# Order of TensorE's work in the steady steps of a window-attention kernel: attention groups ahead of first-layer groups, and one small product moved up

## The chip, the cores and the metric

The kernel runs on one core of one Trainium2 chip. The metric is the device time in microseconds. Before the change it was 338.09 us, the median of 3 runs (336.73 to 339.00).

## The reference, cut to what matters

The input is 8 images of 128 channels by 32 by 32 in float32. Two blocks follow one another.

- The first is a window transformer block. Each image is cut into 16 windows of 8 by 8 tokens. Tokens are normalised over the channels, projected to queries, keys and values for 8 heads of width 16, and softmax attention runs inside each window; its output is projected and added to the input. Then every token is normalised again, goes through a two-layer perceptron (128 to 256, silu, 256 to 128), and the result is added.
- The second is a linear attention block over all 1024 tokens of an image: q, k and v of width 64, `(q k) / N` times v with no softmax, an output projection and the input added. Since nothing non-linear stands between these products, the kernel works with a matrix M of 128 by 128 for each image, made from keys and values, and a column d: the output is M times the tokens plus d.

## The kernel before, in words

The work unit is half an image: 512 tokens, 8 windows, treated as four pairs of windows p = 0 to 3. A step handles several halves at once: half b is in its attention, half a (the next) in its projections, next_a in its first normalisation, half c (the one before) in its output projection, second normalisation and first layer, and the half called tail in its second layer and its keys and values. An even step has b on the first half of an image, an odd step on the second. The loop runs seven even steps of the common form (`even_step`) and six odd ones (`odd_step`), after a prologue and a first and second step of their own, and ahead of an epilogue. Image products of stage d (the matrix M and the output) run in odd steps, for the image before.

Each engine has its order of work written out by hand, one function for each step and engine. Within an engine all is in order; between engines there are only semaphores. The orders of ScalarE (lines 1330 and 1352), GpSimd (600 and 611) and SP (458 and 466) are of the same kind as those that the change touches, TensorE's (983 and 1010) and VectorE's (1690 and 1722).

The names that matter:

- `b_score` (TensorE, 739): scores of all four pairs, for the row maxima. In an even step it stands behind a wait for the first output half to be read from its bank, at the end of the odd step's list.
- `b_scoreT(b, p)` (TensorE, 765): transposed scores of pair p, six products in fp32r and four bfloat16 products that take the row maximum off, into the one bank p_scoreT. For p = 0 in even steps it waits until ScalarE has read the second output half, which uses the same bank. `b_exp` (ScalarE, 1216) makes the probabilities.
- `b_attn(b, p)` (TensorE, 792): sixteen small products, weights of 64 columns. It waits for the probabilities and for VectorE's normalisation `b_norm(b, p-1)` (1526) of the pair before, since the pairs share the bank p_attn.
- `a_v` (TensorE, 728): values; `a_q`, `a_k`: queries and keys; `a_transpose`: transposes of the input.
- `c_transpose` (810), `c_project` (822): o is transposed, ScalarE reads it (`c_o`, 1240), VectorE makes the remainder (`c_o`, 1538), and the projection takes both.
- `c_fc1(c, 0)` and `c_fc1(c, 1)` (TensorE, 841): the two halves of the first layer, three passes each (`three_passes`, 650). For each of them ScalarE makes two activations (`c_silu`, 1252). The second one waits for `c_kv` of VectorE (1575), which evacuates keys and values of the tail.
- `d_kvT` (869), `d_mT` (887), `d_final` (895) on TensorE: the keys-values product of an image, its matrix M, and the two output halves, the second one into p_scoreT. VectorE's `d_mT` (1593) splits M into two parts. `d_out` (ScalarE, 1263) reads each output half.

ScalarE's order at the end of an odd step is: silu of the first group, output half 0, silu of the second group, output half 1; at the start of the next step `c_o`, a table load and the first exponential.

Of the kernel before, what the change touches and what calls it, by code (L numbers as in the profile page):

```python
# [130 lines left out]
def build(nc, x, ln1_g, ln1_b, in_w, in_b, out_w, out_b, ln2_g, ln2_b, fc1_w, fc1_b, fc2_w, fc2_b,  # L131
          wq, bq, wk, bk, wv, bv, wo, bo, out):
    ctx = ExitStack()
    with ctx:
# [514 lines left out]
        def _(pe):  # L649
# [48 lines left out]
            def a_transpose(h):  # L698
                pe.wait_ge(*x_landed(h))
                if h.follows(2):  # L700
                    pe.wait_ge(xn_tok_set, h.n(1))
                for t in range(4):
                    last = pe.transpose(norm_banks(h)[0][:, C * t:C * t + C], x_of(h)[:, C * t:C * t + C], ident[:])  # L703
                last.then_inc(xT_ready, 1)
# [23 lines left out]
            def a_v(h):  # L728
                pe.wait_ge(xn_full, h.n())
                if h.follows(2):  # L730
                    pe.wait_ge(q_high, h.n())
                    pe.wait_ge(q_low, h.n())
                for p in range(PAIRS):
                    last = pe.matmul(v_bank(h)[:, C * p:C * p + C], xn[:, C * p:C * p + C], wv_cols[:],  # L734
                                     start=True, stop=True)
                last.then_inc(v_ready, 1)
# [55 lines left out]
            def b_attn(h, p):  # L792

                pe.wait_ge(probs_ready[p], h.n())
                if p == 0:
                    pe.wait_ge(v_dma, h.n(times=16 * 4))
                    if h.follows(1):
                        pe.wait_ge(o_tok_ready[PAIRS - 1], h.n(1))
                else:
                    pe.wait_ge(o_tok_ready[p - 1], h.n())  # L800
                for j in range(QUADS):
                    for win in range(2):
                        last = pe.matmul(p_attn[64 * win:64 * win + 64, 2 * VB * j:2 * VB * (j + 1)],  # L803
                                         probs[:, p % 2, win, j, :],
                                         vd[:, h.par, 2 * p + win, :, :, j].rearrange("row a d -> row (a d)"),
                                         start=True, stop=True)
                last.then_inc(attn_ready[p], 1)
# [33 lines left out]
            def c_fc1(h, t):  # L841
                pe.wait_ge(yn_high, h.n())
                pe.wait_ge(yn_low, h.n())
                if t == 1 and not h.early and not h.late:
                    if h.follows(1):
                        pe.wait_ge(kv_kept, h.n(1))
                    else:
                        pe.wait_ge(ob_kept, 1)
                three_passes(c_banks(h)[t][:, h.cols], [weights(F1_ + t)], [(yn_h[:, h.cols], yn_l[:, h.cols])]
                             ).then_inc(fc1_ready[t], 1)  # L850
# [18 lines left out]
            def d_kvT(loop, c, tiles=range(8)):  # L869

                pe.wait_ge(kv_kept, loop.halves(c) - 1 if tiles[-1] < 7 else loop.halves(c))
                dst = d_bank(loop, c)
                if loop.follows(c - 1) and dst is p_d:
                    pe.wait_ge(fin_kept[0], loop.image(c - 1))
                for n in tiles:
                    tile = kv_tok[:, n // 4, n % 4]
                    side = slice(E * (n % 2), E * (n % 2) + E)
                    last = pe.matmul(dst[side, 0:E], tile[:, E:2 * E], tile[:, 0:E], start=n < 2, stop=n > 5)  # L878
                if tiles[-1] == 7:
                    last.then_inc(kvT_ready, 1)  # L880
# [6 lines left out]
            def d_mT(loop, c):  # L887
                pe.wait_ge(bT_kept, loop.image(c))
                if not loop.follows(c - 1):
                    pe.wait_ge(w_late_dma, 16 * W_LATE_LOADS)  # L890
                dst = d_bank(loop, c)
                pe.matmul(dst[:, 0:C], wq_rows[:], bT[:], start=True, stop=True)
                pe.matmul(dst[:, C:C + 1], bT[:], col(BQ, rows=E), start=True, stop=True).then_inc(mT_ready, 1)
# [89 lines left out]
            def even_step(loop, more):  # L983
                b, a, next_a, c, tail = loop.half(0), loop.half(1), loop.half(2), loop.half(-1), loop.half(-2)
                b_score(b, True)
                c_transpose(c)
                b_scoreT(b, 0)
                c_fc2(tail)
                c_project(c)
                b_scoreT(b, 1)  # L990
                scores_read(b)
                a_back(a)
                c_yT(c)
                if more:
                    a_transpose(next_a)
                c_kv(tail)
                b_attn(b, 0)
                b_scoreT(b, 2)
                a_q(a)
                a_k(a)  # L1000
                b_attn(b, 1)
                c_back(c)
                b_scoreT(b, 3)
                b_attn(b, 2)
                a_v(a)
                c_fc1(c, 0)
                b_attn(b, 3)
                c_fc1(c, 1)

            def odd_step(loop):  # L1010
                b, a, next_a, c, tail = loop.half(1), loop.half(2), loop.half(3), loop.half(0), loop.half(-1)
                b_score(b, True)
                c_transpose(c)
                b_scoreT(b, 0)
                c_project(c)
                c_fc2(tail)
                b_scoreT(b, 1)
                c_yT(c)
                scores_read(b)
                a_back(a)  # L1020
                c_kv(tail)
                b_attn(b, 0)
                a_transpose(next_a)
                b_scoreT(b, 2)
                d_kvT(loop, -1)
                a_q(a)
                a_k(a)
                b_scoreT(b, 3)
                d_bT(loop, -1)
                c_back(c)  # L1030
                b_attn(b, 1)
                d_mT(loop, -1)
                a_v(a)
                b_attn(b, 2)
                c_fc1(c, 0)
                d_final(loop, -1, 0, p_d)
                c_fc1(c, 1)
                d_final(loop, -1, 1, p_scoreT)
                b_attn(b, 3)
                pe.wait_ge(fin_kept[0], loop.image(-1))  # L1040

            def step_even(loop, more, c):
# [379 lines left out]
        def _(dve):  # L1422
# [267 lines left out]
            def even_step(loop, more):  # L1690
                b, a, next_a, c, tail = loop.half(0), loop.half(1), loop.half(2), loop.half(-1), loop.half(-2)
                b_max(b, 0)
                b_widen(b, 0)
                b_max(b, 1)
                c_o(c)
                b_widen(b, 1)
                b_max(b, 3)
                b_widen(b, 3)
                b_max(b, 2)
                c_y1(c)  # L1700
                c_y2(tail)
                c_stats(c)
                c_aggregate(c)
                a_xn(a)
                if more:
                    a_stats(next_a)
                b_norm(b, 0)
                if more:
                    a_aggregate(next_a)
                c_norm(c)  # L1710
                b_norm(b, 1)
                a_q(a)
                a_k(a)
                c_yn(c)
                c_kv(tail)
                b_norm(b, 2)
                if more:
                    a_norm(next_a)
                b_norm(b, 3)
                a_k_low_block(a)  # L1720

            def odd_step(loop):
                b, a, next_a, c, tail = loop.half(1), loop.half(2), loop.half(3), loop.half(0), loop.half(-1)
                b_max(b, 0)
                b_widen(b, 0)
                c_o(c)
                b_max(b, 1)
                b_widen(b, 1)
                b_max(b, 2)
                b_max(b, 3)  # L1730
                c_y1(c)
                c_y2(tail)
                c_stats(c)
                c_aggregate(c)
                c_kv(tail)
                b_widen(b, 3)
                a_xn(a)
                a_stats(next_a)
                c_norm(c)
                a_aggregate(next_a)  # L1740
                d_kvT(loop, -1)
                b_norm(b, 0)
                a_q(a)
                d_bT(loop, -1)
                a_k(a)
                b_norm(b, 1)
                c_yn(c)
                d_mT(loop, -1)
                b_norm(b, 2)
                a_norm(next_a)  # L1750
                a_k_low_block(a)
                b_norm(b, 3)
# [88 lines left out]
```

## Time and profile before

| what | value |
|---|---|
| median of 3 runs | 338.09 us (336.73 to 339.00) |
| the profiled execution | 338.72 us, of which the span on the core is 336.9 us |
| mean granted TensorE clock | 0.989 |
| busy share of the span | TensorE 95%, its weight loads 80%, VectorE 81%, ScalarE 71%, GpSimd 49% |
| chain that ended last | 80% TensorE, 2% issue, 1% ScalarE, 1% VectorE |

How to read it: the span is the time from the first to the last instruction, and the profiled execution adds what lies around it. In the timeline a start is followed by a duration; since TensorE's products overlap, the time that a group takes out of TensorE's list is the distance from its start to the start of the next. "Idle before" stands in brackets with what ended it. "issue" is idle time in which the profile shows no wait.

### The profile page before, as it was taken

The numbers are of one execution on the slowest core, as the hardware profiler recorded it, in microseconds if no ns is written. First come the engines' busy times: TensorE is split into PE (matmuls) and PEld (weight loads), VectorE is DVE, ScalarE is ACT, GpSimd is POOL, SyncE is SP. The second block draws the span as 40 slices with busy tenths as digits, with TensorE's granted clock in tenths as the row PEclk, the third lists the DMA queues.
The fourth block names the chain that finished last, engine by engine and source line by source line (L and its number), as shares of the span: only waits on it lengthen the run. The fifth ranks groups of instructions, "written<-read, shape, count | busy, mean of one in ns | idle before, by whom it ended". The sixth has DMA issues, their size and how long they took to land.

```text
span 336.9 us, 9735 instructions
## 1 busy us (share of the span) xinstructions
PE 319.2 (95%) x3442; PEld 269.1 (80%) x3442; DVE 273.5 (81%) x851; ACT 238.5 (71%) x446; POOL 165.5 (49%) x177
## 2 busy tenths in 40 slices
PE   6979898999999999999999999999999999999695
PEld 6868777878887888878888888878888888878484
DVE  4586798988798987988798987988698987878662
ACT  5366487777959588776959688776959688775452
POOL 6604755637346354737446363646436363643511
PEclk9979999999999999999999999999999999999989
DMA  4333022131503123130413124130413123120002
GB/s 140 70 92 104 3 62 64 43 89 25 140 27 87 42 70 120 40 87 24 133 38 80 47 65 126 31 99 18 116 58 79 51 56 103 27 68 3 0 33 94
DMA packets 31887, 22.36 MB, mean 66 GB/s; under 512 B 22432, under 2 KB 23776, under 8 KB 31840
## 3 DMA queue, kind: packets, MB, share of 16 engines
q1 hardware_dynamic: 31744, 21.62, 23.6%
q8 instruction: 28, 0.46, 0.6%
q14 instruction: 19, 0.16, 0.2%
q10 hardware_dynamic: 96, 0.13, 0.2%
HBM read 4.95 MB, written 4.19 MB: 27 GB/s over the span
## 4 chain that ended last, share of the span: by engine, by line
PE 80%; issue 2%; ACT 1%; DVE 1%; DVEq 0%; ACTq 0%
PE p_c L655 16%; PE p_scoreT L784 13%; PE p_attn L803 11%; PE p_x L655 9%; PE p_scoreT L788 4%; PE p_x L734 4%; PE p_c L864 4%; PE p_x L756 3%; PE p_c L838 2%; PE p_c L819 2%; PE p_c L832 2%; PE p_x L703 2%; PE p_x L712 2%; PE p_scoreT L655 2%; PE p_x L878 1%
## 5 line engine op out<-in xcount | busy, mean ns | idle before, releaser
L1223 ACT ACTIVATE probs<-p_scoreT 128x512 f32<-128x512 f32 x64 | 37.8, 590 | 43.3 <-PE p_scoreT L788 42.4
L549 POOL TENSOR_TENSOR hid_l<-hid,hid_h 128x512 fp32r<-128x512 f32 x30 | 40.0, 1346 | 39.6 <-ACT hid_h L1258 33.6
L1514 DVE TENSOR_REDUCE row_max<-p_x 128x8 f32<-128x512 f32 x64 | 43.2, 683 | 8.4 <-PE p_x L756 8.4
L803 PEld LDWEIGHTS p_attn<-vd,probs 128*64 128x64 f32 x1024 | 36.2, 139 | 13.1 <-issue 9.5
L803 PE MATMUL p_attn<-vd,probs 128*64 128x34 f32 x1024 | 45.6, 245 | 0.1
L784 PE MATMUL p_scoreT<-qd_h,kd_h 128*128 128x256 f32 x128 | 39.7, 310 | 0.7 <-issue 0.7
L520 POOL TENSOR_SCALAR x_res<-x_in,out_b 128x256 f32<-128x256 f32 x28 | 25.7, 928 | 29.0 <-issue 29.0
L531 POOL TENSOR_SCALAR rstd<-mv 128x4 f32<-128x4 f32 (+1 forms) x33 | 7.5, 228 | 61.1 <-DVE mv L1455 61.1
L533 POOL TENSOR_TENSOR rstd<-rstd,minus_half 128x4 f32<-128x4 f32 (+1 forms) x33 | 35.3, 1070 | 2.8
L784 PE MATMUL p_scoreT<-qd_l,kd_h 128*128 128x256 f32 x128 | 36.2, 282 | 0.0
L784 PE MATMUL p_scoreT<-qd_h,kd_l 128*128 128x256 f32 x128 | 36.0, 281 | 0.0
L541 POOL TENSOR_SCALAR kd_l<-k_l,head_a 128x512 fp32r<-128x512 f32 x15 | 23.6, 1576 | 20.8 <-issue 10.8
L784 PEld LDWEIGHTS p_scoreT<-qd_h,kd_h 128*128 128x128 f32 x128 | 24.4, 191 | 4.2 <-issue 1.1
L1532 DVE RECIPROCAL inv_sum<-p_attn 128x8 f32<-128x8 f32 x64 | 12.9, 201 | 18.2 <-PE p_attn L803 18.2
L788 PE MATMUL p_scoreT<-neg_ident,max_wide 128*128 128x128 bf16 x256 | 25.4, 222 | 0.3 <-DVE max_wide L1523 0.3
L784 PEld LDWEIGHTS p_scoreT<-qd_l,kd_h 128*128 128x128 f32 x128 | 24.5, 191 | 1.0
L784 PEld LDWEIGHTS p_scoreT<-qd_h,kd_l 128*128 128x128 f32 x128 | 24.3, 190 | 0.0
L1207 ACT ACTIVATE kd_h<-k_h,head_a 128x512 fp32r<-128x512 f32 x32 | 22.8, 717 | 1.3
L1523 DVE CAST max_wide<-row_max 128x512 bf16<-128x512 f32 x49 | 22.0, 449 | 1.2
L554 POOL TENSOR_TENSOR y_l<-y,y_h 128x512 fp32r<-128x512 f32 x15 | 19.2, 1280 | 7.4 <-ACT y_h L1238 7.4
L1258 ACT ACTIVATE hid_h<-p_c,fc_b 128x512 fp32r<-128x512 f32 x30 | 20.7, 691 | 2.6 <-PE p_c L655 2.6
L1463 DVE TENSOR_SCALAR xn_tok<-p_x,mv,rstd 128x128 f32<-128x128 f32 x60 | 20.4, 402 | 1.6 <-POOL rstd L533 1.6
(247 smaller groups left out, 882.5 us busy)
## 6 DMA issues: line engine op xcount, KB each, us to landing
qd_l<-q_l SPq DMA_DIRECT2D x64, 64.0 KB, 2.0
vd<-v_tok SPq DMA_DIRECT2D x64, 64.0 KB, 2.2
qd_h<-q_h SPq DMA_DIRECT2D x62, 64.0 KB, 2.0
out<-out_sb SPq DMA_DIRECT2D x15, 256.0 KB, 2.6
x_in<-in_x SPq DMA_DIRECT2D x14, 256.0 KB, 3.0
x_first<-in_x SPq DMA_DIRECT2D x2, 256.0 KB, 2.7
fc_rows<-in_L_conv_fc_w SPq DMA_DIRECT2D x2, 128.0 KB, 2.5
out<-out_sb SPq DMA_DIRECT2D x2, 128.0 KB, 2.2
```

The lines of the kernel that those rows point to most:

```text
L520: last = pool.tensor_scalar(in_windows(x_res[:, h.par, :], v), in_rows(x_of(h), v), out_b2[:, 0:1], None, ALU.add)
L533: pool.tensor_tensor(out_[:, tiles], out_[:, tiles], minus_half[:, tiles], ALU.pow).then_inc(out_set, 1)
L541: pool.tensor_scalar(kd_l[:, h.par, :, 0, :], k_l[:].bitcast(F32).rearrange("p (win k) -> p win k", k=KEYS), head_a[:, 0:1], None, ALU.mul ...
L549: pool.tensor_tensor(hid_l[:, t], hid[:, t], hid_h[:, t].bitcast(F32), ALU.subtract).then_inc(hid_low[t], 1)
L655: last = pe.matmul(dst, weight, moving_part, start=k == 0, stop=k == len(passes) - 1)
L784: pe.matmul(dst[:, win], kd[:, h.par, window], qd[:, h.par, :, KEYS * window:KEYS * (window + 1)], start=win == 0 and k == 0, stop=False, ...
L788: last = pe.matmul(dst[:, :, j, :], max_wide[:, p, 2 * j:2 * j + 2, :], neg_ident[:], start=False, stop=j == QUADS - 1, skip_group_check=True)
L803: last = pe.matmul(p_attn[64 * win:64 * win + 64, 2 * VB * j:2 * VB * (j + 1)], probs[:, p % 2, win, j, :], vd[:, h.par, 2 * p + win, :, : ...
L1207: act.activation(kd_h[:, h.par, :, a, :], k_h[:].bitcast(F32).rearrange("p (win k) -> p win k", k=KEYS), ACT.Copy, scale=head_a[:, a:a + 1 ...
L1223: act.activation(probs[:, p % 2], p_scoreT[:].rearrange("row (win j q) -> row win j q", win=2, j=QUADS), ACT.Exp, scale=SCORE_SCALE).then_ ...
L1514: dve.tensor_reduce(row_max[:, p].rearrange("row (j a) -> row j a", a=2), score(p).rearrange("row j (a k) -> row j a k", a=2), AXIS_X, ALU.max
L1523: dve.tensor_copy(max_wide[:, p], row_max[:, p].unsqueeze(2).to_broadcast([128, HEADS, KEYS])).then_inc(max_wide_ready[p], 1)
```

## The change: what it does

On TensorE, in even steps the last attention group goes ahead of the first layer's first group. In odd steps the third attention group goes ahead of the values, the fourth ahead of the first layer's first group (before, it ended the step), and the keys-values product `d_kvT` goes ahead of the third transposed scores. On VectorE, the third normalisation goes ahead of `c_kv` in even steps and ahead of `d_mT` in odd steps. No other engine's order is changed.

```diff
@@ TensorE, even_step @@
                 b_attn(b, 2)
                 a_v(a)
+                b_attn(b, 3)
                 c_fc1(c, 0)
-                b_attn(b, 3)
                 c_fc1(c, 1)
@@ TensorE, odd_step @@
                 a_transpose(next_a)
+                d_kvT(loop, -1)
                 b_scoreT(b, 2)
-                d_kvT(loop, -1)
                 a_q(a)
@@ TensorE, odd_step @@
                 b_attn(b, 1)
                 d_mT(loop, -1)
+                b_attn(b, 2)
                 a_v(a)
-                b_attn(b, 2)
+                b_attn(b, 3)
                 c_fc1(c, 0)
                 d_final(loop, -1, 0, p_d)
                 c_fc1(c, 1)
                 d_final(loop, -1, 1, p_scoreT)
-                b_attn(b, 3)
                 pe.wait_ge(fin_kept[0], loop.image(-1))
@@ VectorE, even_step @@
                 c_yn(c)
+                b_norm(b, 2)
                 c_kv(tail)
-                b_norm(b, 2)
@@ VectorE, odd_step @@
                 c_yn(c)
+                b_norm(b, 2)
                 d_mT(loop, -1)
-                b_norm(b, 2)
```

## Rows read from the trace of the kernel before

**Rows 1.** The page, part 1: engine, busy us (share of the span), instructions.
```profile
PE 319.2 (95%) x3442; PEld 269.1 (80%) x3442; DVE 273.5 (81%) x851; ACT 238.5 (71%) x446; POOL 165.5 (49%) x177
```

**Rows 2.** The list of waits: engine, line, releaser, us in total, times, longest us.
```profile
PEld p_attn L803 <- issue: 9.5, 32, 0.4
...
PE p_c L655 <- issue: 2.2, 6, 0.4
```

**Rows 3.** Timeline of TensorE, an odd step's tail: start us, us, operation, count.
```profile
159.76 0.48 PE L892 MATMUL p_x<-bT,wq_rows 64*128 64x128 f32 x2
...
160.29 1.16 PE L734 MATMUL p_x<-wv_cols,xn 128*128 128x128 f32 x8
161.38 0.71 PE L803 MATMUL p_attn<-vd,probs 128*64 128x34 f32 x16
162.02 0.50 PE L655 MATMUL p_c<-yn_h,wh 128*128 128x512 f32 x1
...
162.82 0.40 PE L655 MATMUL p_x<-y_h,m_h 128*128 128x512 f32 x1
...
165.00 0.71 PE L803 MATMUL p_attn<-vd,probs 128*64 128x34 f32 x16
165.64 0.91 PE L756 MATMUL p_x<-kd_h,q_h 32*128 32x128 f32 x32
166.48 0.66 PE L819 MATMUL p_c<-ident,o_tok 128*128 128x128 f32 x4
167.06 0.35 PE L784 MATMUL p_scoreT<-qd_h,kd_h 128*128 128x256 f32 x1
```

**Rows 4.** Timeline of TensorE, the even step's tail and the odd step's start.
```profile
179.72 1.16 PE L734 MATMUL p_x<-wv_cols,xn 128*128 128x128 f32 x8
180.64 0.48 PE L655 MATMUL p_c<-yn_h,wh 128*128 128x512 f32 x1
...
182.15 0.50 PE L655 MATMUL p_c<-yn_h,wh 128*128 128x512 f32 x1
...
183.04 0.91 PE L756 MATMUL p_x<-kd_h,q_h 32*128 32x128 f32 x32
183.88 0.66 PE L819 MATMUL p_c<-ident,o_tok 128*128 128x128 f32 x4
184.29 0.36 PE L784 MATMUL p_scoreT<-qd_h,kd_h 128*128 128x256 f32 x1
...
186.00 0.47 PE L655 MATMUL p_c<-o_h,wh 128*128 128x512 f32 x1 [0.39 <-issue]
```

**Rows 5.** Timeline of ScalarE, the odd step.
```profile
156.63 0.69 ACT L1183 ACTIVATE q_h<-p_x,qkv_b 128x512 fp32r<-128x512 f32 x1 [0.91 <-PE p_x L655]
...
163.05 0.68 ACT L1258 ACTIVATE hid_h<-p_c,fc_b 128x512 fp32r<-128x512 f32 x1
...
164.19 0.84 ACT L1269 ACTIVATE out_sb<-p_x,d_col 128x256 f32<-128x256 f32 x2
...
166.04 0.88 ACT L1269 ACTIVATE out_sb<-p_scoreT,d_col 128x256 f32<-128x256 f32 x2
```

**Rows 6.** Timeline of VectorE, the odd step's start.
```profile
185.21 0.69 DVE L1542 TENSOR_TENSOR o_l<-p_c,o_h 128x512 fp32r<-128x512 f32 x1
```

**Rows 7.** Timeline of ScalarE, the even step's tail and the odd step's start.
```profile
182.09 0.68 ACT L1258 ACTIVATE hid_h<-p_c,fc_b 128x512 fp32r<-128x512 f32 x1
...
184.57 0.60 ACT L1244 ACTIVATE o_h<-p_c 128x512 fp32r<-128x512 f32 x1
```

**Rows 8.** Timeline of VectorE, the odd step.
```profile
152.94 0.69 DVE L1581 TENSOR_TENSOR kv_tok<-p_c,kv_bias 128x512 f32<-128x512 f32 x1
...
160.13 0.29 DVE L1534 TENSOR_TENSOR o_tok<-p_attn,inv_sum 128x128 f32<-128x128 f32 x1
...
161.51 0.29 DVE L1604 TENSOR_TENSOR m_l<-mT,m_h 128x128 fp32r<-128x128 f32 x1
```

**Rows 9.** Timeline of TensorE, the odd step, the transposes of the input.
```profile
153.47 0.66 PE L703 MATMUL p_x<-ident,x_in 128*128 128x128 f32 x4
```

## The prediction

> **What bounds the kernel now.** I read the page first: TensorE is busy for 95% of the span [rows 1], so the time is the length of TensorE's own list of work plus the few places where that list stands still. The list of waits, kept to TensorE, names those places: the longest that repeats is 2.2 us in six pieces ahead of a product into p_c, and the weight loads of the attention groups stand for 9.5 us in 32 pieces with no releaser [rows 2]. Then I read the timeline engine by engine through one odd and one even step in the middle of the span, since the steps repeat each other.
>
> In the odd step's tail the reader should look at the hand-over to the next even step. The last group of attention starts at 165.00 (the three products before it take 162.82 to that point), the scores at 165.64, four transposes at 166.48, the first transposed score only at 167.06 [rows 3]. The four transposes took 0.58 us there; the same four took 0.41 (183.88 to 184.29) where an odd step begins [rows 4]. The difference, 0.17, is a wait: the even step's first transposed score may not start before ScalarE has read the second output half out of the same bank, and that read starts at 166.04 and takes 0.88, to 166.92 [rows 5]. ScalarE's chain from the first hidden activation (163.05) over the first output half (164.19) to there is 3.87 us of unbroken work [rows 5], and it starts 0.23 after the first layer's first three products have been issued (162.82) [rows 3]. So here ScalarE's chain, hung on the first layer's first group, is as long as TensorE's path, with 0.64 of attention in TensorE's path as its cover.
>
> At the other hand-over, even to odd, TensorE idles 0.39 ahead of the projection at 186.00 [rows 4]. That is released by VectorE's remainder of o, 185.21 plus 0.69 [rows 6], which had to wait for ScalarE's read of o, 184.57 plus 0.60 [rows 7].
>
> **Prices of the seams.** A sixteen-matmul attention group takes 0.64 (161.38 to 162.02). Between a group of full-array products and an attention group there is a gap: the eight value products take 0.92 ahead of the first layer [rows 4] and 1.09 ahead of attention [rows 3], so 0.17. A first-layer group after attention with another three-pass product behind it takes 0.80 (162.02 to 162.82) [rows 3]; after attention with the scores behind it 0.89 [rows 4]. The three products from 162.82 to the scores at 165.64, less the attention's 0.64, take 2.18, so with p for a plain group, e for the entry and s for the exit, 3p+s is 2.18, p+e is 0.80, p+e+s is 0.89: s 0.09, e 0.10, p 0.70.
>
> The row shows that the loads for attention don't go ahead of the products before them (9.5 us of standing weight loads [rows 2]). The Trainium skill (TensorE: Matmul & The Clock Gate, What each phase is for) says that the queue pulls weight loads ahead of running products; by that alone the 0.17 would be no switch but a wait, and the new order would save it, which is a rival below. Its page on tiling (TensorEngine Tiling (Array Packing), Key Properties) says that changing the tiling mode drains the engine; the 0.17 agrees with that one.
>
> **The change, step by step.** Nothing is added or removed; no DMA is issued elsewhere, and the orders of ScalarE, GpSimd and SP stay as they are.
>
> *Even step, last attention ahead of the first layer's first group.* Before, from the value products to the scores: 179.72 to 183.04, 3.32 [rows 4]. After: values 1.09, attention 0.64, first layer 0.80 and then p+s, 0.79: 3.32. TensorE gains nothing. But the first layer's first group now ends at 179.72+1.09+0.64+0.80 = 182.25, and with the 0.2 lag ScalarE's first activation starts at 182.45 instead of 182.09; four of them at 0.57 (1.14 a pair, 163.05 to 164.19 [rows 5]) end at 184.73, where ScalarE reads o at 184.57 today [rows 7]. So the read of o, its remainder and the projection come 0.16 later. Bounds 0 and 0.36 (the whole delay). I take 0.16, for seven even steps: 1.1 us. The VectorE move takes the keys-values evacuation, whose like lasts 0.69 [rows 8], out of the way of the third normalisation, which the attention now waits for at 180.81; so nothing waits there, and the evacuation is wanted only by the first layer's second group, at 182.25.
>
> *Odd step, third and fourth attention.* The third group moves ahead of the value products. It needs VectorE's second normalisation, which ends at 160.13+0.29 = 160.42 [rows 8]; a VectorE release takes some 0.1 (185.90 to 186.00), so it starts at about 160.5, where the value products start at 160.29 today [rows 3]: 0.2 of new wait, because these products were its cover. Then attention 0.64, values 1.09, attention 0.64: the first layer's first group starts at 162.87 instead of 162.02, 0.85 later. The matrix steps on VectorE that go behind the third normalisation end at 161.51+0.29 = 161.80 today, 1.4 after the second normalisation [rows 8]. From the third group's end (161.14), with a normalisation as late behind it as the second one today (160.42 against 159.76, 0.66) and the whole 1.4 after that, they would end by 163.2, ahead of the output product at 163.67. They are hidden; if not, that product would stand until then.
>
> From the first layer on, ScalarE's chain of 3.87 and its lag move along by 0.85 whole, while TensorE's way to the first transposed score lost the attention (0.64). TensorE arrives at 163.67+2.18+0.84+0.41 = 167.10; the bank is read out for it at 167.06+0.85 = 167.91. The wait there grows from 0.17 to 0.8: what left the path behind the first layer is paid again as a wait, and what came in front of the first layer is paid in full. Floor 0.64 (no new wait at the third group), ceiling 0.85. I take 0.75, for six pairs: 4.5 us, because some of the wait may cover the row maxima that the next products also wait for. What is queued behind the wait is all of the even step; the input load behind SP's store of the output is later by the same amount as its reader, so it costs nothing.
>
> *Odd step, keys-values product ahead of the third scores.* It would start at 153.47+0.41+0.17 = 154.05 [rows 9]; its input is ready at 152.94+0.69 = 153.63 [rows 8], so it doesn't wait. Two seams before, two after: I take 0, bounds plus and minus one seam, 0.17, for six: 1.0 us either way. The exponential behind the third scores comes later by the group that passes it, under 0.7, and ScalarE idles 0.91 ahead of its next work [rows 5]: hidden.
>
> **Sum.** 4.5+1.1 = 5.6 us on the profiled execution's 338.72, 344.3. That execution is 0.63 above the median of 338.09, so I expect a median of 343.7. By the floors (3.8+0-1.0) it is 340.9, by the ceilings (5.1+2.5+1.0) 346.7.
>
> **Rivals.**
> *A, ScalarE isn't what holds the first transposed score.* Then the 0.17 is TensorE's own, only TensorE's sum counts: 0.2 of new wait in six odd steps, 1.3 us, 339.4. For it: the gap is small. Against it: it is missing where an odd step starts, and it ends 0.14 after the read-out. Chance 0.17.
> *B, no switch cost ahead of attention.* The pull-ahead of weight loads is real and the 0.17 a wait that the new order loses: the even step saves 0.17, the odd step's first layer is late by 0.68 instead of 0.85, so 6 x 0.6 less 7 x 0.17 plus nothing for the projection: +2.4, 340.5. Against it: the value products are the same in both places and what attention needs is old by then. Chance 0.07.
> *C, faster.* The earlier normalisations bring both hand-overs in: the last one frees VectorE before the scores, the read of o comes earlier, and the 0.17 and 0.39 both vanish: 6 x 0.56 = 3.4, 334.7. It decides if o's transposes wait for the last normalisation today; in the timeline they follow the scores without a gap (165.64 to 166.48, as 183.04 to 183.88), which speaks against it. Chance 0.06.
>
> **How the numbers follow.** The forecast has 0.70; of it 0.06 falls short of 1%, which is about what a measurement of this kernel can tell from no change (341.5). Slower 0.64; within 1% 0.06+0.17+0.07 = 0.30; faster 0.06. The forecast's own range is 341 to 346.7. To hold A and B and leave out C and the ends, the range goes from 337.6 to 346.5.
>
> **What would show it.** In the changed profile: the odd step's first layer starts some 0.85 later after the second attention group; ScalarE stands idle ahead of the first hidden activation; the transposes ahead of the even step's first transposed score are followed by a gap of 0.7 or more; the idle ahead of the projection in odd steps grows from 0.39 towards 0.55; value products take 1.09 in even steps too. The prediction is wrong if the even step's first transposed score follows its transposes within 0.5, or if values ahead of attention take 0.92.

## The result, and the profile after

The changed kernel takes 344.68 us, the median of 4 runs (342.86 to 346.17), against 337.64 for 4 runs of the kernel before: 1.0191 times as long, 95% interval 1.0152 to 1.0229. 343.7 was forecast, in a range of 337.6 to 346.5, with 0.64 on slower. The profiled execution is 344.94 us with a span of 343.1, so 6.2 above that of before in both; the medians are 7.0 apart, and the sum had said 5.6.

The page's first part (engine, busy us, share, instructions) and the split of the chain that ended last:

```profile
PE 320.5 (93%) x3442; PEld 269.9 (79%) x3442; DVE 277.7 (81%) x851; ACT 239.2 (70%) x446; POOL 164.9 (48%) x177
...
PE 70%; ACT 5%; issue 5%; DVE 3%; DVEq 0%; ACTq 0%
```

TensorE does the same work [rows 1] in a longer span, and the shares of ScalarE and VectorE in the chain, 1% each before, have grown. The list of waits, kept to TensorE, names two that were not there before, six times each, and a third that was 0.3 us in two pieces before:

```profile
PE p_scoreT L784 <- ACT out_sb L1269: 2.9, 6, 0.5
...
PE p_attn L803 <- DVE o_tok L1534: 1.2, 6, 0.2
PE p_scoreT L788 <- DVE max_wide L1523: 1.2, 5, 0.2
```

TensorE's timeline in the odd step's tail, to hold beside [rows 3] (start us, us, operation). This odd step's scores start at 146.15, those of [rows 3] at 144.88.

```profile
161.28 0.48 PE L892 MATMUL p_x<-bT,wq_rows 64*128 64x128 f32 x2
...
162.08 0.72 PE L803 MATMUL p_attn<-vd,probs 128*64 128x34 f32 x16 [0.20 <-DVE o_tok L1534]
162.73 1.16 PE L734 MATMUL p_x<-wv_cols,xn 128*128 128x128 f32 x8
163.81 0.71 PE L803 MATMUL p_attn<-vd,probs 128*64 128x34 f32 x16
164.46 0.50 PE L655 MATMUL p_c<-yn_h,wh 128*128 128x512 f32 x1
...
165.26 0.40 PE L655 MATMUL p_x<-y_h,m_h 128*128 128x512 f32 x1
...
167.51 0.90 PE L756 MATMUL p_x<-kd_h,q_h 32*128 32x128 f32 x32
168.34 0.66 PE L819 MATMUL p_c<-ident,o_tok 128*128 128x128 f32 x4
169.48 0.36 PE L784 MATMUL p_scoreT<-qd_h,kd_h 128*128 128x256 f32 x1 [0.48 <-ACT out_sb L1269]
```

From the step's scores the first layer starts 18.31 us in (17.14 before), the next scores 21.36 (20.76), the first transposed score 23.33 (22.18). The last attention group is gone from ahead of the scores, and still the transposed score is 1.15 later: it now stands 1.14 behind the start of the transposes, where it stood 0.58 [rows 3]. ScalarE's timeline of the same tail, beside [rows 5]:

```profile
163.92 0.60 ACT L1214 ACTIVATE v_tok<-p_x 128x512 f32<-128x512 f32 x1 [0.35 <-PE p_x L734]
164.41 0.71 ACT L1207 ACTIVATE kd_h<-k_h,head_a 128x512 fp32r<-128x512 f32 x1
165.46 0.69 ACT L1258 ACTIVATE hid_h<-p_c,fc_b 128x512 fp32r<-128x512 f32 x1 [0.33 <-PE p_c L655]
...
166.61 0.84 ACT L1269 ACTIVATE out_sb<-p_x,d_col 128x256 f32<-128x256 f32 x2
...
168.47 0.88 ACT L1269 ACTIVATE out_sb<-p_scoreT,d_col 128x256 f32<-128x256 f32 x2
```

The reader is to see the two brackets: ScalarE now stands idle twice, for the values and for the first layer, ahead of the chain that releases the even step; that chain is 165.46 to 169.35, 3.89 long, as before (3.87).

The even step's tail and the odd step's start, TensorE, ScalarE and VectorE, beside [rows 4], [rows 7] and [rows 6]:

```profile
182.12 1.16 PE L734 MATMUL p_x<-wv_cols,xn 128*128 128x128 f32 x8
183.20 0.71 PE L803 MATMUL p_attn<-vd,probs 128*64 128x34 f32 x16
183.84 0.50 PE L655 MATMUL p_c<-yn_h,wh 128*128 128x512 f32 x1
...
185.44 0.91 PE L756 MATMUL p_x<-kd_h,q_h 32*128 32x128 f32 x32
...
187.88 0.40 PE L788 MATMUL p_scoreT<-neg_ident,max_wide 128*128 128x128 bf16 x4 [0.23 <-DVE max_wide L1523]
188.58 0.47 PE L655 MATMUL p_c<-o_h,wh 128*128 128x512 f32 x1 [0.31 <-issue]
```

```profile
184.85 0.69 ACT L1258 ACTIVATE hid_h<-p_c,fc_b 128x512 fp32r<-128x512 f32 x1 [0.23 <-PE p_c L655]
...
187.15 0.61 ACT L1244 ACTIVATE o_h<-p_c 128x512 fp32r<-128x512 f32 x1
```

```profile
187.13 0.69 DVE L1523 CAST max_wide<-row_max 128x512 bf16<-128x512 f32 x1
187.79 0.69 DVE L1542 TENSOR_TENSOR o_l<-p_c,o_h 128x512 fp32r<-128x512 f32 x1
```

From the values to the scores 182.12 to 185.44, 3.32, the same as before. From the scores to the projection 3.14, where it was 2.96. The idle time right ahead of the projection is shorter than before, 0.31 against 0.39, but TensorE now also waits 0.23 a little earlier, for `max_wide`: 0.54 in all.

The steps repeat, so the length of one (from its scores to the next step's, read off TensorE's timeline of each kernel, the usual value of its six) is a finer measure than the time of a run. One odd step each in the changed kernel, e2, e8, e9 and e11 is 0.2 to 1.0 us longer than the others and doesn't count. The "widening" is VectorE's `max_wide`: each row maximum is copied out to all keys of its row in bfloat16, for the products that take it off.

| kernel | odd step, us | even step, us | pair | against before |
|---|---|---|---|---|
| before | 20.76 | 17.40 | 38.16 | |
| changed | 21.35 | 17.94 | 39.29 | +1.13 |
| e1 even step's edits alone | 20.93 | 17.40 | 38.33 | +0.17 |
| e2 odd step's attention edits alone | 21.10 | 17.93 | 39.03 | +0.87 |
| e4 keys-values product alone | 20.82 | 17.38 | 38.20 | +0.04 |
| e3 changed, last group back at the end | 21.05 | 17.78 | 38.83 | +0.67 |
| e10 e3, keys ahead of values on ScalarE | 21.06 | 17.39 | 38.45 | +0.29 |
| e5 changed, another bank | 21.36 | 17.95 | 39.31 | +1.15 |
| e6 changed, widening from PSUM | 21.35 | 17.81 | 39.16 | +1.00 |
| e7 changed, both | 21.35 | 17.53 | 38.88 | +0.72 |
| e8 before, widening from PSUM | 20.88 | 17.52 | 38.40 | +0.24 |
| e9 before, last group behind both first layers | 20.98 | 17.25 | 38.23 | +0.07 |
| e11 before, first layer ahead of the third group | 20.77 | 17.37 | 38.14 | -0.02 |
| e12 e11, a block of keys on VectorE | 20.77 | 17.25 | 38.02 | -0.14 |

The three parts of the change (e1, e2, e4) add up to 1.08 of the 1.13; six pairs of 1.13 are 6.8 us, near the 7.0 of the medians. The profiled execution shows only 6.2 because it reached the scores of its first odd step at 67.59, that of before at 68.57; of that stretch the change touches one even step alone, which is 18.37 long in both.

### The profile page after: what moved, and what is told of

Same layout as the page of the kernel before. It is cut to its first block, busy times and chain, and to the rows that moved or that the text cites. A ratio compares the mean times of both kernels' runs of the same rounds, so it can differ in the third digit from the quotient of the medians.

```text
span 343.1 us, 9735 instructions
## 1 busy us (share of the span) xinstructions
PE 320.5 (93%) x3442; PEld 269.9 (79%) x3442; DVE 277.7 (81%) x851; ACT 239.2 (70%) x446; POOL 164.9 (48%) x177
## 4 chain that ended last, share of the span: by engine, by line
PE 70%; ACT 5%; issue 5%; DVE 3%; DVEq 0%; ACTq 0%
PE p_c L655 15%; PE p_scoreT L784 12%; PE p_attn L803 11%; PE p_x L655 7%; PE p_scoreT L788 4%; PE p_x L734 4%; PE p_c L864 4%; ACT out_sb L1269 3%; PE p_c L838 2%; ACT hid L1260 2%; PE p_c L832 2%; PE p_x L703 2%; PE p_x L756 2%; PE p_x L712 2%; PE p_x L878 1%
## 5 line engine op out<-in xcount | busy, mean ns | idle before, releaser
L1523 DVE CAST max_wide<-row_max 128x512 bf16<-128x512 f32 x49 | 27.1, 553 | 1.2
L1260 ACT ACTIVATE hid<-p_c,fc_b 128x512 f32<-128x512 f32 x30 | 20.7, 692 | 0.0
```

Source lines behind the costliest of these rows:

```text
L1260: act.activation(hid[:, t, h.cols], c_banks(h)[t][:, h.cols], ACT.Silu, bias=fc1_b2[:, t:t + 1]).then_inc(hid_full[t], 1)
L1523: dve.tensor_copy(max_wide[:, p], row_max[:, p].unsqueeze(2).to_broadcast([128, HEADS, KEYS])).then_inc(max_wide_ready[p], 1)
```

## The experiments

**The parts of the change.** Edit of e1, to the kernel before:

```diff
                 a_v(a)
+                b_attn(b, 3)
                 c_fc1(c, 0)
-                b_attn(b, 3)
@@ VectorE @@
+                b_norm(b, 2)
                 c_kv(tail)
-                b_norm(b, 2)
```

Expected: 

> The kernel before with the even step's two edits alone (TensorE and VectorE). Theory (ScalarE's chain behind the first layer's first group): TensorE's own time from the value products to the scores stays at 3.96 us from the third attention group on; the projection of the next odd step starts 3.14 us after that step's scores instead of 2.96, seven times: +1.2 us, ratio 1.002 to 1.006. Rival (the even step carries half of the loss, as the even step's own length of +0.53 per pair might suggest): +3 us, 1.009 or more.

Measured 1.0046 (1.0015 to 1.0077); 0.17 a pair, all of it in the odd step that follows. The theory holds; the even step's longer 17.94 in the changed kernel comes from the odd step's edits, not from its own.

Edit of e2, to the kernel before (VectorE's `b_norm(b, 2)` goes ahead of `d_mT` too):

```diff
                 d_mT(loop, -1)
+                b_attn(b, 2)
                 a_v(a)
-                b_attn(b, 2)
+                b_attn(b, 3)
                 c_fc1(c, 0)
...
-                b_attn(b, 3)
```

Expected: 

> The kernel before with the odd step's third and fourth attention group moved, and VectorE's matrix step behind the third normalisation; the even step and the keys-values product stay. Theory: the first layer's first group comes 0.9 us later in the odd step and the next even step's first transposed score with it, six times: +5.4 us, ratio 1.013 to 1.018; the wait behind the transposes of o in even steps is 0.7 us. Rival (cover by ScalarE doesn't matter, only the 0.2 wait of the third group does): +1.3 us, 1.004.

Measured 1.0189 (1.0149 to 1.0229), just above the theory's range; by the steps 0.87 a pair or 5.2 us in six, inside it. Its third group waits 0.20 for VectorE, as forecast, and the even step's first transposed score stands 1.15 behind the start of the transposes of o instead of 0.41 (the theory's wait of 0.7). How the 0.87 is shared between the two groups this run can't tell.

Edit of e4: `d_kvT(loop, -1)` ahead of `b_scoreT(b, 2)`.

Expected: 

> The kernel before with the keys-values product moved ahead of the third transposed scores in odd steps, nothing else. One look for its trace: from the transposes of the input to the query products 2.23 us instead of 2.15 (theory: two seams in both orders, 0.08 dearer), no wait ahead of the keys-values product. By the time +0.5 us, which one run can't tell from nothing. Rival: the order saves a seam, 2.0 us or less.

From the input's transposes to the queries 2.23 (151.13 to 153.36): the theory's value. By the step it costs 0.04.

**Which move of the odd step.** Edit of e3, to the changed kernel:

```diff
-                b_attn(b, 3)
                 c_fc1(c, 0)
                 d_final(loop, -1, 0, p_d)
                 c_fc1(c, 1)
                 d_final(loop, -1, 1, p_scoreT)
+                b_attn(b, 3)
```

Expected: 

> The changed kernel with one edit undone: in odd steps the last attention group ends the step again; all else stays changed. Theory: the cover behind the first layer is back, what is left is 0.18 of the projection, 0.08 of the keys-values product and about 0.1 of the third group's wait per pair, +2.2 us against the kernel before, ratio 1.004 to 1.009, so 4 to 5 us faster than the changed kernel. Rival (the last group's place isn't the cause, the third group's new wait and the VectorE moves are): ratio stays at 1.015 or above.

Measured 1.0158 (1.0116 to 1.0200), in the rival's region; by the steps the loss is 6 times 0.67, 4.0 us or 1.2%, between the theory and the rival. The pair fell by 0.46 only; the even step still lost 0.38. So my theory of a chain that starts with the first layer was not the whole. ScalarE's timeline of this kernel says why:

```profile
161.48 0.60 ACT L1214 ACTIVATE v_tok<-p_x 128x512 f32<-128x512 f32 x1 [0.34 <-PE p_x L734]
161.97 0.71 ACT L1207 ACTIVATE kd_h<-k_h,head_a 128x512 fp32r<-128x512 f32 x1
162.59 0.68 ACT L1258 ACTIVATE hid_h<-p_c,fc_b 128x512 fp32r<-128x512 f32 x1
...
165.57 0.88 ACT L1269 ACTIVATE out_sb<-p_scoreT,d_col 128x256 f32<-128x256 f32 x2
```

The first layer is there in time, but ScalarE isn't: it waited for the values, which now come behind the third attention group, and then had values, keys and silu to do without a break. The read of the second output half is late by that, and TensorE waits again for it:

```profile
166.60 0.35 PE L784 MATMUL p_scoreT<-qd_h,kd_h 128*128 128x256 f32 x1 [0.33 <-ACT out_sb L1269]
```

The new theory, that the chain starts at the values, was put to a test that leaves TensorE's and VectorE's orders alone. Edit of e10, to e3, on ScalarE:

```diff
-                a_v(a)
                 a_k_block(a, 0)
+                a_v(a)
                 c_silu(c, 0)
```

Expected: 

> The changed kernel with the last attention group of odd steps back at the end (38.83 us for an odd and an even step), and in ScalarE's odd step the first block of keys ahead of the values. Theory: what that kernel lost beside the even step and the keys-values product (0.42 a pair) is that the values come later behind the third attention group, and ScalarE's chain of values, keys, silu starts idle for 0.34; with the keys first that idle time is filled: 38.5 us a pair, 2 us faster than without the swap. Rival (the 0.2 wait of the third group on TensorE and VectorE's order are the cause): 38.8, unchanged.

Measured 38.45 a pair, and 1.0060 (1.0031 to 1.0090) of the kernel before:

```profile
163.25 0.71 ACT L1207 ACTIVATE kd_h<-k_h,head_a 128x512 fp32r<-128x512 f32 x1
163.87 0.58 ACT L1214 ACTIVATE v_tok<-p_x 128x512 f32<-128x512 f32 x1
164.40 0.69 ACT L1258 ACTIVATE hid_h<-p_c,fc_b 128x512 fp32r<-128x512 f32 x1
```

No bracket is left: the idle time is filled with the keys, which had been ready, and 0.38 a pair comes back though the third group's wait and VectorE's order are untouched. The even step is at 17.39 again. What is left of the pair's loss, 0.29, is 0.17 of the projection (e1), 0.04 of the keys-values product (e4) and 0.08. So the third group costs its time through the values and ScalarE, not through its own wait.

Edit of e9, to the kernel before: `b_attn(b, 3)` between `c_fc1(c, 1)` and `d_final(loop, -1, 1, p_scoreT)`.

Expected: 

> The kernel before with one edit: in odd steps the last attention group leaves the end of the step but stays behind both first-layer groups (ahead of the second output half). Theory (the loss comes from what is put ahead of the values and of the first layer, not from leaving the end): ScalarE's chain starts when it did, one seam more on TensorE, an odd and an even step together take 38.2 us by the trace against 38.16, ratio 0.998 to 1.004. Rival (the last group is needed as cover right ahead of the scores): as in the changed kernel's odd tail, 38.6 or more, 1.008.

Measured 0.9995 (0.9955 to 1.0034), 38.23 a pair (one odd step of its profile, 21.98, is left out of that). The group may leave the end of the step at next to no cost, as long as it stays behind the first layer. It isn't the end that mattered, but what the group was put in front of.

**What holds the even step back in the changed kernel.** Edit of e5: the second output half goes to the bank of the attention.

```diff
-                d_final(loop, -1, 1, p_scoreT)
+                d_final(loop, -1, 1, p_attn)
```

ScalarE reads it there, the wait for that read moves from `b_scoreT(b, 0)` to the even step's `b_attn(b, 0)`, and the product waits for VectorE's last normalisation instead of the last probabilities.

Expected: 

> The changed kernel with the second output half of the odd step in the bank of the attention (free there, since the last attention group is now early) instead of the bank of the transposed scores, so that the even step's first transposed score needs no wait for ScalarE's read of it. Theory 1 (the bank alone holds the step): the transposed score follows the transposes of o at 0.41, the step gets back 0.7 us, six times: 4 us faster than the changed kernel, ratio to the kernel before 1.007. Theory 2 (two more things hang on the same ScalarE chain: GpSimd's remainder of the second hidden group, which locks out VectorE's widening of the row maxima, and the second layer that needs that remainder): the six score products start early but the bfloat16 products behind them stand until the widened maxima, as late as in the changed kernel; less than 0.1 us per pair comes back, under 1 us, ratio 1.016 to 1.020.

Measured 1.0205 (1.0158 to 1.0252), 39.31 a pair: nothing came back. TensorE's timeline:

```profile
169.01 0.66 PE L819 MATMUL p_c<-ident,o_tok 128*128 128x128 f32 x4
169.42 0.36 PE L782 MATMUL p_scoreT<-qd_h,kd_h 128*128 128x256 f32 x1
...
171.04 0.40 PE L786 MATMUL p_scoreT<-neg_ident,max_wide 128*128 128x128 bf16 x4 [0.65 <-DVE max_wide L1523]
```

The transposed score follows the transposes at 0.41, so the wait for the bank is gone, and the same time is lost six products later, on VectorE's widened row maxima. What made those late is to be seen in the changed kernel too, in a pair of rows of VectorE and GpSimd:

```profile
169.20 1.10 DVE L1523 CAST max_wide<-row_max 128x512 bf16<-128x512 f32 x1
```

```profile
168.75 1.27 POOL L549 TENSOR_TENSOR hid_l<-hid,hid_h 128x512 fp32r<-128x512 f32 x1 [0.60 <-issue]
```

The widening takes 0.43 where nothing is in its way (169.58 in e3's trace); here it takes 1.10 and ends 0.28 behind the end of GpSimd's remainder of the second hidden group, which itself hangs on ScalarE's silu. Theory 2 holds for the widening; whether the second layer's wait for the remainder binds as well, this run doesn't show.

Edit of e6 and e7 (e7 with e5's too): the widening of the first pair as a maximum of the scores in PSUM (where TensorE's output banks are) with the row maximum.

```diff
-                dve.tensor_copy(max_wide[:, p], row_max[:, p].unsqueeze(2).to_broadcast([128, HEADS, KEYS])
+                dve.tensor_tensor(max_wide[:, p].rearrange("row (j a) k -> row j a k", a=2),
+                                  score(p).rearrange("row j (a k) -> row j a k", a=2),
+                                  row_max[:, p].rearrange("row (j a) -> row j a", a=2).unsqueeze(3)
+                                  .to_broadcast([128, QUADS, 2, KEYS]), ALU.max).then_inc(max_wide_ready[p], 1)
```

Expected of e6: 

> The changed kernel with VectorE's widening of the first pair's row maxima done as a maximum of the scores in PSUM with the row maximum (the same value), so that it isn't a copy from SBUF to SBUF that a GpSimd instruction can lock out. Theory 2: it takes 0.7 us instead of 1.10 in even steps, but the first transposed score still starts with the read-out of the bank (169.5 in the changed kernel's trace), so the bfloat16 products start within 0.1 us of where they did: 0 to -0.6 us, ratio 1.016 to 1.020. If the widening alone held the step: -0.45 x 6 = -2.7 us, 1.011.

Expected of e7: 

> Both edits of the two kernels before this one in the changed kernel. Theory 2: with the bank free and the widening not locked out, the next limit is the second layer's wait for GpSimd's remainder of the second hidden group, which lets it start some 0.45 us earlier than in the changed kernel: -0.45 x 6 = -2.7 us, ratio about 1.011, while each edit alone gives under 1 us. Theory 1 (bank alone): the same as the bank edit, 1.007 in both.

Measured 1.0161 (1.0121 to 1.0201) and 1.0144 (1.0091 to 1.0197). The intervals overlap; the pairs are sharper: alone the bank gives 0, the widening 0.13 (0.8 us in six, a little more than the 0.6 expected), together 0.41, and six times 0.41 is 2.5 us, near the 2.7 that was expected of both. In e7 TensorE, VectorE and GpSimd show what comes next:

```profile
167.67 0.66 PE L819 MATMUL p_c<-ident,o_tok 128*128 128x128 f32 x4
168.08 0.36 PE L782 MATMUL p_scoreT<-qd_h,kd_h 128*128 128x256 f32 x1
...
169.27 0.40 PE L786 MATMUL p_scoreT<-neg_ident,max_wide 128*128 128x128 bf16 x4 [0.23 <-DVE max_wide L1524]
169.50 0.47 PE L655 MATMUL p_c<-hid_h,wh 128*128 128x512 f32 x1
```

```profile
168.52 0.69 DVE L1524 TENSOR_TENSOR max_wide<-p_x,row_max 128x512 bf16<-128x512 f32 x1
```

```profile
168.07 1.28 POOL L549 TENSOR_TENSOR hid_l<-hid,hid_h 128x512 fp32r<-128x512 f32 x1 [0.60 <-issue]
```

The widening, now 0.69 with GpSimd at work beside it, ends at 169.21, the remainder at 169.35, and the second layer, which needs the remainder and stands behind the bfloat16 products in TensorE's list, starts at 169.50. It follows those products at 0.23, in the kernel before at 0.22 (167.94 to 168.16), so no wait of its own is shown: e7 comes out near the expected number, but not by the limit that was expected. What the even step still loses (17.53 against 17.40) is the price of the widening's slower form, 0.69 where the copy took 0.56 in the kernel before:

```profile
167.32 0.56 DVE L1523 CAST max_wide<-row_max 128x512 bf16<-128x512 f32 x1
```

Two limits at nearly the same place, the bank and the widening, are why no single edit gives the time back.

The same edit in the kernel before was e8.

Expected: 

> The kernel before with the widening edit alone. In its even step the bank is the limit of the first transposed score and the widening ends with it (both within 0.1 us), in odd steps the widening isn't locked out: 0 +- 1 us, ratio 0.997 to 1.003. If the widening held the kernel before more than the bank does: -1 us or more.

Measured 1.0042 (1.0015 to 1.0069), 0.24 a pair, 0.12 in each step: a miss. The widening had taken 0.43 in odd steps and 0.56 in even ones; from PSUM it takes 0.69 in both. In odd steps VectorE's next work, the remainder of o, starts 2.30 behind the scores instead of 2.17, in even steps the bfloat16 products that need the widening start at 2.44 instead of 2.30. I had counted only GpSimd's hold on the copy.

**The other way.** Edit of e11, to the kernel before: `c_fc1(c, 0)` ahead of `b_attn(b, 2)` in odd steps.

Expected: 

> The kernel before with an edit the other way: in odd steps the first layer's first group ahead of the third attention group, right behind the values. Theory: ScalarE is busy without a break from its read of yn on (table load, values, keys), so an earlier first layer doesn't start it earlier: 38.16 us a pair, within 0.1, ratio 0.997 to 1.003. Rival (the first layer alone sets ScalarE's start): 0.17 to 0.25 less a pair, 37.95, -1.3 us.

Measured 1.0012 (0.9982 to 1.0042), 38.14 a pair: as the theory has it. From the odd step's scores the first layer starts at 16.31 instead of 17.14, ScalarE's first silu at 18.15, where it was 18.17.

Edit of e12, to e11, in odd steps:

```diff
@@ ScalarE @@
-                a_k_block(a, 0)
@@ VectorE @@
+                a_norm(next_a)
                 b_norm(b, 2)
-                a_norm(next_a)
                 a_k_low_block(a)
+                a_k_high_block(a)
```

`a_k_high_block` makes on VectorE the block that ScalarE made.

Expected: 

> The kernel of the edit before this one, and ScalarE's first block of keys in odd steps made by VectorE (behind its fourth-block work, ahead of the last normalisation), with the normalisation of the next half ahead of the third attention normalisation. Theory: now ScalarE's chain is 0.6 us shorter and its first layer is there, so the read of the second output half ends 0.4 to 0.6 us earlier, the wait of 0.17 ahead of the even step's first transposed score goes; what is late next is the row maximum: 38.0 us a pair, 1 us faster than the kernel before, ratio 0.994 to 0.999. If VectorE is the next limit (scores wait for its blocks): 38.3 or more.

Measured 0.9989 (0.9958 to 1.0020), 337.63 us against 338.12: not to be told from the kernel before by its time. By the trace the pair is 38.02, 0.14 shorter; the transposed score follows the transposes at 0.42 (166.48 to 166.90), so the wait of 0.17 is gone. It is the only kernel here with a clearly shorter pair.

## Why the prediction was right, point by point

- *Even step, TensorE gains nothing:* 3.32 forecast, 3.32 measured. The value products ahead of attention took 1.08 there, against 0.92 ahead of the first layer, so the seam is a price of the pair of neighbours and not a wait, and rival B is out.
- *Even step, projection 0.16 later:* 0.17 (e1), by the path named: first silu at 184.85, read of o at 187.15 right behind the fourth activation, remainder at 187.79. The sign for it failed by the letter: the idle time ahead of the projection was to grow from 0.39 towards 0.55 and fell to 0.31. The growth is there (0.54), but 0.23 of it stands ahead of the bfloat16 products, since the widening met GpSimd's remainder and took 0.69 instead of 0.43, which the prediction didn't count.
- *Odd step, 0.2 of wait ahead of the third group:* 0.20.
- *First layer 0.85 later:* 0.92 (1.17 less the 0.25 that the step had lost ahead of it). VectorE's release took 0.15 (161.64 plus 0.29, to 162.08) where 0.1 was taken.
- *Even step's transposed score, 0.75 between a floor of 0.64 and a ceiling of 0.85:* 0.87 a pair in e2. This term was mis-sized. I took 0.75 because the row maxima behind might give some back; they gave nothing, since in the new order their widening hangs on ScalarE's chain as well, over GpSimd. Six times 0.12 is 0.7 us, half of the gap between the sum's 5.6 and the 7.0 of the medians. The 6.2 of the profiled executions lies closer to the sum only by the stretch ahead of the first odd step.
- *Keys-values product 0:* 0.04.
- *Rival A* (ScalarE isn't what holds the transposed score): out; the list of waits names ScalarE's read six times, and the time is 5 us above the rival's 339.4. But that read is not the only holder: without it (e5) the widening, late by the same chain, holds the step in its place. *Rival C:* out, both hand-overs grew.

What the prediction's reasoning had wrong is where ScalarE's chain starts, and with it the split inside that term. It hung the chain on the first layer alone and gave the last group 0.64 of the loss and the third group 0.2. The runs put it at 0.46 for the last group (e3) and about 0.4 for the third (e10), which works through the values. ScalarE's timeline of before, ahead of the first silu at 163.05 [rows 5], had it:

```profile
160.56 1.28 ACT L1121 ACT_TABLE_LOAD   x1
...
161.96 0.58 ACT L1214 ACTIVATE v_tok<-p_x 128x512 f32<-128x512 f32 x1
162.44 0.71 ACT L1207 ACTIVATE kd_h<-k_h,head_a 128x512 fp32r<-128x512 f32 x1
```

There is no bracket: ScalarE works through from the table load, and its own work, not the first layer, sets when the chain starts (e11 shows it by a run). No step of the prediction asked what a later start of the values does. The total came out near by luck in part. Where the first layer does set the start, in the changed kernel, the silu follows 0.20 after the group has been issued (165.26 to 165.46); before it was 0.23, so ScalarE's own work and the first layer were level within 0.03. That is why the delay of the first layer, worked out with both moved groups in front of it, was nearly the delay of the chain: 0.91 and 0.88 in e2, counted from the odd step's scores.

## What to carry to other kernels

Ahead of moving work on the bound engine, list what each later group on it feeds, and put work that feeds nobody soon (here the last attention group) behind the groups that start another engine's long chain. Where that other engine is busy without a break up to a hand-over, the path through it can be the bound there, whatever the busy shares say; filling its first idle moment with work that is ready can then give time back without a change of the bound engine's order (0.38 a pair in e10). When a wait is taken away and nothing comes back, look for the next consumer of the same chain.

## What the runs showed of the hardware

VectorE's copy from SBUF to SBUF with a change of type is held while GpSimd runs a subtraction of 128 by 512: it ended 0.28 behind GpSimd's end in the changed kernel (170.02 and 170.30), and again in e5 (1.12 instead of 0.43). In e12 a multiplication by a column, SBUF to SBUF, met the same instruction of GpSimd and took 1.59, where the like of it ahead took 0.48:

```profile
163.42 0.48 DVE L1506 TENSOR_SCALAR kd_l<-k_l,head_a 128x512 fp32r<-128x512 f32 x1
163.81 1.59 DVE L1511 TENSOR_SCALAR kd_h<-k_h,head_a 128x512 fp32r<-128x512 f32 x1
```

```profile
163.82 1.29 POOL L549 TENSOR_TENSOR hid_l<-hid,hid_h 128x512 fp32r<-128x512 f32 x1 [2.49 <-ACT hid_h L1258]
```

It ended at 165.40, 0.29 behind GpSimd's 165.11. The form that reads one operand from PSUM took 0.69 beside a running GpSimd (e7). GpSimd can be the one that is held: in an odd step of the kernel before, the copy, started at 146.57 between two subtractions, took 0.43, and the two took 2.78 together (145.34 to 148.12); with the widening from PSUM they took 2.52 (e8, 145.42 to 147.94). The Trainium skill (SBUF — State Buffer, Who interferes with whom) says that copies, casts and operations with a scalar can enter a mode that needs the port pair shared with GpSimd, which is an exclusive lock for a whole instruction, and that an instruction with at most one SBUF input outside such modes doesn't contend; these numbers agree. The price of avoiding it is the slower form where nothing is in the way (e8).
